# A last addition over 128 half images in 14 chunks, and a process product that alternates between the halves of its output

## The reference

```
h = tok(x)                                   # 64 x 196 x 256
h = h + attn(layernorm(h))
acts = gelu(layernorm(h) @ input_patterns.T).mean(tokens)        # 64 x 2048
input_repr = keep the 256 largest of acts, zero elsewhere
process = gelu(input_repr @ process_input_weights.T)             # 64 x 1024
top 128 of process, softmax -> mix process_values -> 64 x 128
out_acts = gelu(mixed @ output_input_weights.T)                  # 64 x 2048, keep the 256 largest
out = kept out_acts @ output_patterns                            # 64 x 256, one vector per image
h = h + out, the same vector for all 196 tokens of an image
```

## Time and profile before

| what | us |
|---|---|
| median of 3 runs (1791.88 to 1796.01) | 1794.66 |
| profiled execution, its own time | 1792.7 |
| its span, first to last instruction | 1790.7 |
| process product, on the chain | 26.75, from 1583.08 |
| first addition begins | 1739.09 |
| first store is issued | 1741.47 |
| end of the span | 1790.7 |

### The profile page before, as it was taken

One profiled execution on the slowest core, in us unless ns is written; L12 is line 12 of the kernel. 1 busy time (PEld: TensorE's weight loads), 2 busy tenths in 40 slices (PEclk: granted clock), 3 DMA queues, 4 the chain that ended last, 5 costly groups with the idle time before them and its releaser, 6 DMA issues. The chain is left out here.

```text
span 1790.7 us, 32340 instructions
## 1 busy us (share of the span) xinstructions
PE 1523.7 (85%) x10035; PEld 1461.8 (82%) x10035; DVE 1026.3 (57%) x2479; ACT 879.0 (49%) x3121; POOL 107.8 (6%) x240
## 2 busy tenths in 40 slices
PE   1479999999999999999999999999999996572133
PEld 1369999999999999999999999999999996431122
DVE  2365555555555555555555555555555443736776
ACT  1235555555555555555555555555555545511320
POOL 0010000000000000000000000000000000000000
PEclk8699999999999999999999999999999998585567
DMA  5211111111111111111111111111100002485008
GB/s 99 82 54 43 41 39 36 36 36 37 37 37 37 37 37 37 37 36 36 36 36 36 36 36 36 36 37 37 37 24 9 10 13 77 142 203 142 0 22 266
DMA packets 80357, 94.19 MB, mean 53 GB/s; under 512 B 12977, under 2 KB 78513, under 8 KB 79281
## 3 DMA queue, kind: packets, MB, share of 16 engines
q1 hardware_dynamic: 79744, 93.40, 18.8%
q10 hardware_dynamic: 576, 0.35, 0.2%
HBM read 68.01 MB, written 25.69 MB: 52 GB/s over the span
## 5 line engine op out<-in xcount | busy, mean ns | idle before, releaser
L641 ACT ACTIVATE ffn<-ffn 128x196 f32<-128x196 f32 x1024 | 332.7, 325 | 254.4 <-PE ffn L557 253.9
L557 PE MATMUL ffn<-x_t_hi,pat_w_hi 128*128 128x392 f32 x1024 | 362.0, 353 | 1.7 <-DVE x_t_lo L765 1.7
L557 PE MATMUL ffn<-x_t_lo,pat_w_hi 128*128 128x392 f32 x1024 | 350.1, 342 | 0.0
L557 PE MATMUL ffn<-x_t_hi,pat_w_lo 128*128 128x392 f32 x1024 | 348.7, 340 | 0.0
L490 PE MATMUL gen<-qkvu_w_hi,h_t_hi 128*98 128x256 f32 x768 | 216.2, 282 | 5.4 <-ACT q_t L599 5.1
L490 PE MATMUL gen<-qkvu_w_hi,h_t_lo 128*98 128x256 f32 x768 | 216.2, 282 | 0.0
L490 PE MATMUL gen<-qkvu_w_lo,h_t_hi 128*98 128x256 f32 x768 | 215.7, 281 | 0.0
L641 ACT ACTIVATION_READ_ACCUMULATOR ffn<-ffn 128x1 f32 x1024 | 196.2, 192 | 0.0
L557 PEld LDWEIGHTS ffn<-x_t_hi,pat_w_hi 128*128 128x128 f32 x1024 | 192.7, 188 | 2.0 <-DVE x_t_lo L765 2.0
L557 PEld LDWEIGHTS ffn<-x_t_lo,pat_w_hi 128*128 128x128 f32 x1024 | 193.1, 189 | 0.0
L557 PEld LDWEIGHTS ffn<-x_t_hi,pat_w_lo 128*128 128x128 f32 x1024 | 192.8, 188 | 0.0
(11 more groups left out here) (192 smaller groups left out, 2753.4 us busy)
## 6 DMA issues: line engine op xcount, KB each, us to landing
raw<-in_x_dram SPq DMA_DIRECT2D x768, 49.0 KB
h_dram<-h SPq DMA_DIRECT2D x128, 98.0 KB
process_nat<-ocess_input_weights_dram SPq DMA_DIRECT2D x8, 1024.0 KB, 4.8
process_t<-h_dram SPq DMA_DIRECT2D x4, 1568.0 KB
out_dram<-process_t SPq DMA_DIRECT2D x8, 784.0 KB
h_early<-h_dram SPq DMA_DIRECT2D x3, 1568.0 KB
out_dram<-h_early SPq DMA_DIRECT2D x6, 784.0 KB
pat_nat<-_ffn_input_patterns_dram SPq DMA_DIRECT2D x1, 2048.0 KB, 8.3
```

Source lines behind the costliest of these rows:

```text
L557: last = pe.matmul(fb[f % FFN_BANKS][:, 0:T2], a[:, d, f * P:(f + 1) * P], b[:, d, :], start=n == 0, stop=n == 3 * s.halves - 1)
L641: last = act.activation(cols, cols, ACT.Gelu, accum_out=gelu_sum[:, par, at:at + 1])
```

## The change

- The tokens of the last addition are laid out over 128 partitions. Partition p holds one half image, 98 tokens that lie side by side in DRAM. The work is cut into 14 chunks of 7 tokens, so a chunk is 128 partitions x 1792 numbers, and each partition's 7168 bytes are one run on both sides of the transfer.
- The homes hold 4, 2 and 8 chunks, in the same three buffers and behind the same waits.
- PE spreads the routed vectors once: `both_halves` is now 128 columns, each image twice, and two matmuls (high and low part) put every half image's vector on its partition in bank `rp0`. DVE reads it from that bank for all 14 chunks.
- SP loads a chunk per DMA and stores a chunk per DMA, 14 of each (before 8 and 16).
- The process product does both halves of a tile before it goes to the next tile.

```diff
-        EARLY = 3 * GROUP
-        h2_early = sb("h2_early", [s.tile, EARLY, 2 * D])
-        homes = [h2_early[:], process_nat[0:s.tile].rearrange("p a b -> p (a b)").rearrange("p (n d) -> p n d", d=2 * D),
-                 process_t[0:s.tile].rearrange("p a b -> p (a b)").rearrange("p (n d) -> p n d", d=2 * D)]
+        TOKENS = s.tokens // 2
+        CHUNK = 7
+        CHUNKS = TOKENS // CHUNK
+        EARLY = 4
+        h2_early = sb("h2_early", [P, EARLY, CHUNK * D])
+        in_nat = process_nat[:].rearrange("p a b -> p (a b)")[:, 0:2 * CHUNK * D]
+        in_turned = process_t[:].rearrange("p a b -> p (a b)")[:, 0:(CHUNKS - EARLY - 2) * CHUNK * D]
+        homes = [h2_early[:], in_nat.rearrange("p (n y) -> p n y", n=2),
+                 in_turned.rearrange("p (n y) -> p n y", n=CHUNKS - EARLY - 2)]
...
-        both_halves = sb("both_halves", [P, B], F32R)
+        both_halves = sb("both_halves", [P, B, 2], F32R)
...
-            for first in range(0, B, GROUP):
-                n, at = h2_home(first)
+            def rows(dram, g):
+                return dram.rearrange("(p t) d -> p (t d)", t=TOKENS)[:, g * CHUNK * D:(g + 1) * CHUNK * D]
+
+            for g in range(CHUNKS):
+                n, at = h2_home(g)
...
-                sp.dma_start(tiles(homes[n][:, at:at + GROUP], GROUP), rows(h2_dram, first, GROUP)).then_inc(h2_in[n], 16)
-            STORE = 4
-            for first in range(0, B, STORE):
-                n, at = h2_home(first)
-                sp.wait_ge(added, (first + STORE) // 2)
-                sp.dma_start(rows(out, first, STORE), tiles(homes[n][:, at:at + STORE], STORE)).then_inc(
-                    out_stored[first // STORE % 4], 16)
+                sp.dma_start(homes[n][:, at], rows(h2_dram, g)).then_inc(h2_in[n], 16)
+            for g in range(CHUNKS):
+                n, at = h2_home(g)
+                sp.wait_ge(added, g + 1)
+                sp.dma_start(rows(out, g), homes[n][:, at]).then_inc(out_stored[g % 4], 16)
...
-                    last = pe.matmul(out, chosen_t[:, at * P + u * B:at * P + (u + 1) * B], weights(t),
-                                     start=n == 0, stop=n == tiles - 1)
+                    for v, out in enumerate(outs):
+                        last = pe.matmul(out, chosen_t[:, at * P + u * B:at * P + (u + 1) * B], weights(t, v),
+                                         start=n == 0, stop=n == tiles - 1)
...
-            for u in range(2):
-                last = chosen_product(prod[0][half_rows(u), :], IN_T,
-                                      lambda t: process_t[:, t, u * NARROW:(u + 1) * NARROW], 0 if u == 0 else None)
-            last.then_inc(product, 1)
+            chosen_product([prod[0][half_rows(v), :] for v in range(2)], IN_T,
+                           lambda t, v: process_t[:, t, v * NARROW:(v + 1) * NARROW], 0).then_inc(product, 1)
...
-            for f in range(B // 2):
-                if f >= 4:
-                    pe.wait_ge(added, f - 3)
-                for g in range(2 * f, 2 * f + 2):
-                    one = both_halves[:, g:g + 1].to_broadcast([P, s.tile])
-                    for n, part in enumerate(routed):
-                        last = pe.matmul(prod[f % 4][0:s.tile, g % 2 * D:(g % 2 + 1) * D], one, part[:],
-                                         start=n == 0, stop=n == 1)
-                last.then_inc(spread, 1)
+            for n, part in enumerate(routed):
+                last = pe.matmul(prod[0][:, 0:D], both_halves[:].rearrange("p b u -> p (b u)"), part[:],
+                                 start=n == 0, stop=n == 1)
+            last.then_inc(spread, 1)
...
-            for f in range(B // 2):
-                n, at = h2_home(2 * f)
-                if at == 0:
-                    dve.wait_ge(h2_in[n], 16 * (homes[n].shape[1] // GROUP))
-                tiles = homes[n][:, at:at + 2].rearrange("t g (u d) -> t g u d", u=2)
-                dve.wait_ge(spread, f + 1)
-                vectors = prod[f % 4][0:s.tile, :].rearrange("t (g d) -> t g d", g=2)
-                dve.tensor_tensor(tiles, tiles, vectors.unsqueeze(2).to_broadcast([s.tile, 2, 2, D]),
+            dve.wait_ge(spread, 1)
+            for g in range(CHUNKS):
+                n, at = h2_home(g)
+                dve.wait_ge(h2_in[n], 16 * homes[n].shape[1])
+                dve.tensor_tensor(by_token(homes[n][:, at]), by_token(homes[n][:, at]), to_all(prod[0][:, 0:D]),
                                   ALU.add).then_inc(added, 1)
```

More of the change, by code:

```diff
@@ L858, in route @@
         STAGE = 2 * ROUNDS
-        GROUP = 8
         process_nat = sb("process_nat", [P, 2, s.n_in])
@@ L880, in route @@
         reached_too = sb("reached_too", [P, HALF], BF16)
-        EARLY = 3 * GROUP
         UNROLL = 4
-        h2_early = sb("h2_early", [s.tile, EARLY, 2 * D])
-        homes = [h2_early[:], process_nat[0:s.tile].rearrange("p a b -> p (a b)").rearrange("p (n d) -> p n d", d=2 * D),
-                 process_t[0:s.tile].rearrange("p a b -> p (a b)").rearrange("p (n d) -> p n d", d=2 * D)]
-        assert sum(home.shape[1] for home in homes) == B
+        TOKENS = s.tokens // 2
[7 more added lines that the diff above has]
+                 in_turned.rearrange("p (n y) -> p n y", n=CHUNKS - EARLY - 2)]
+        assert CHUNK * CHUNKS == TOKENS and sum(home.shape[1] for home in homes) == CHUNKS
         def h2_home(g):
@@ L943, in half_rows, with by_token, to_all @@
             return slice(n * B, (n + 1) * B)
+        def by_token(ap):
+            return ap.rearrange("p (t d) -> p t d", d=D)
+        def to_all(ap):
+            return ap.unsqueeze(1).to_broadcast([P, CHUNK, D])
         block = ctx.enter_context(nc.Block())
@@ L972, in _ @@
                     sp.wait_ge(product, 1)
-                sp.dma_start(tiles(homes[n][:, at:at + GROUP], GROUP), rows(h2_dram, first, GROUP)).then_inc(h2_in[n], 16)
-            STORE = 4
-            for first in range(0, B, STORE):
-                n, at = h2_home(first)
-                sp.wait_ge(added, (first + STORE) // 2)
-                sp.dma_start(rows(out, first, STORE), tiles(homes[n][:, at:at + STORE], STORE)).then_inc(
-                    out_stored[first // STORE % 4], 16)
+                sp.dma_start(homes[n][:, at], rows(h2_dram, g)).then_inc(h2_in[n], 16)
[3 more added lines that the diff above has]
+                sp.dma_start(rows(out, g), homes[n][:, at]).then_inc(out_stored[g % 4], 16)
             for n in range(4):
-                sp.wait_ge(out_stored[n], 16 * (B // STORE // 4))
+                sp.wait_ge(out_stored[n], 16 * len(range(n, CHUNKS, 4)))
         @block.gpsimd
@@ L1036, in turn_chosen, with chosen_product @@
                     last.then_inc(chosen_turned, 1)
-            def chosen_product(out, tiles, weights, done):
+            def chosen_product(outs, tiles, weights, done):
                 half = tiles // 2
@@ L1043, in chosen_product @@
                     u, at = divmod(t, half)
-                    if done is not None and n % 8 == 0:
+                    if n % 8 == 0:
                         pe.wait_ge(chosen_kept, done + n // 8 + 1)
-                    last = pe.matmul(out, chosen_t[:, at * P + u * B:at * P + (u + 1) * B], weights(t),
-                                     start=n == 0, stop=n == tiles - 1)
+                    for v, out in enumerate(outs):
+                        last = pe.matmul(out, chosen_t[:, at * P + u * B:at * P + (u + 1) * B], weights(t, v),
+                                         start=n == 0, stop=n == tiles - 1)
                 return last
@@ L1078, in _ @@
             pe.wait_ge(copied, fills + out_fills)
-            chosen_product(prod[2][0:B, 0:s.d_pv + 1], PROC_T, lambda t: values[:, t, :], 2).then_inc(product, 1)
+            chosen_product([prod[2][0:B, 0:s.d_pv + 1]], PROC_T, lambda t, v: values[:, t, :], 2).then_inc(product, 1)
             pe.wait_ge(result, 2)
@@ L1140, in _ @@
             act.wait_ge(masks_made, 6)
-            act.activation(both_halves[:], same_image[:, 0:B], ACT.Copy)
+            act.activation(both_halves[:], same_image[:, 0:B].unsqueeze(2).to_broadcast([P, B, 2]), ACT.Copy)
             for n in range(STAGE):
```

## The result

The changed kernel takes 1768.01 us, against 1794.01 before on the same chip: a ratio of 0.9847 (95% interval 0.9823 to 0.987), 26 us faster. (One execution of it took 2637 us with PE at a mean clock of 0.55; the ratio leaves it out, and the median hardly feels it.) The forecast was 1766 and faster, with a range of 1762 to 1775. The profiled execution took 1768.29 us, its span 1766.6.

A forecast was written before the change was run, and what follows sets the result against it. It took the process product on the chain of waits and the stream of stores at the tail as the bounds. Terms of -11.8, -0.2, -0.4 and -16.2 us sum to -28.6, giving 1766 us, range 1762 to 1775.

The forecast's parts named there:

- What bounds the kernel: In the route, the process product sits alone on the chain of waits; the tail is bound by the stores.
- Step 1: Process product: alternating halves pair two instructions per step, 33 steps, 26.75 to 15.0 us, a term of -11.8 us.
- the seam rows: Profile rows between the product's two passes, showing extra weight loads per 0.43 us step; they would allow 32 steps, 14.6 us.
- Steps 2 and 3: Spread of vectors, 128 matmuls to 2, -0.2 us; additions 1.93 us each, first store waiting for one, -0.4 us.
- not the bound: Claim that DVE's additions, delivering 475 GB/s, outpace anything the transfers did in the trace.
- Step 4: Stream of stores at the tail: 410 GB/s instead of 279, 47.5 to 31.3 us, a term of -16.2 us.
- The rival of a lower ceiling for writes near 361: Stores limited to 361 GB/s: stream 35.6 us, 4.3 us more, 1770 us; chance 0.17.
- The rival that only partitions count: Stores at 279 to 325 GB/s, stream 46 to 39.5 us, 1774 to 1781 us; chance 0.10.
- The slower rival: Scattered writes at 98 KB pitch fall to 193 GB/s, stream 66.6 us, 1801 us in all; chance 0.03.
- The sum: All terms together -28.6 us: span 1790.7 to 1762.1, profiled execution 1764.1, median 1766 us.
- the third case: In the list of chances, stores at 279 to 325 GB/s, 1774 to 1781 us; chance 0.10.
- the second: In the list of chances, the write ceiling near 361 GB/s, 1770 us; chance 0.17.

The follow-up runs named there:

- tail alone: The changed kernel with the process product in two passes again, lower half then upper: median 1778.03 us, ratio 0.9903 to the kernel before.
- short first store: The changed kernel with chunk 0 added and stored in two pieces, 2 and 5 tokens: median 1763.39 us, ratio 0.9829 to the kernel before.
- product alone: The kernel before with only the process product alternating between halves: median 1783.63 us, ratio 0.9938 to the kernel before.
- 112 partitions: The changed kernel with tokens on 112 partitions, 16 chunks of 7 tokens, runs of 7 KB: median 1769.48 us, ratio 0.986 to the kernel before.
- PE busy ahead of product: The changed kernel with five extra matmuls into a free bank before the process product: median 1761.94 us, ratio 0.9819 to the kernel before.
- few columns: The short first store kernel, with every addition after the first piece covering one token only: median 1763.94 us, ratio 0.9826 to the kernel before.

## Why the prediction was right

**What bounds the kernel** held: between the kernel with the tail alone and the changed kernel the product differs by 11.05 us and the other two pieces by 0.3 or less, so the product's time comes off the end one for one, and the end is the stream of stores.

**Step 1** had -11.8, measured -11.05 in the profile, and -10.9 to -12.1 over all runs with paired halves and no extra matmuls. The pairing was right. Two things inside it were off and partly cancelled. There are 32 steps and not 33 (13.9 us at the upper level is 32 x 0.43 and the drain), as the seam rows had allowed; by the prediction's own terms that is 14.7 us and not the 14.6 it gives. And the steps at the lower level are 2 to 4.5, not always 2: the changed kernel's profile had some 4, which is (15.70 - 13.9) / 0.43. When the level rises differs from one execution to the next.

**Steps 2 and 3** had -0.2 and -0.4. From the product's end to the first addition it is 0.6 less, of which 0.2 are the two matmuls and 0.26 the output product's clock; the first store comes 0.33 earlier. The additions follow each other at 1.93 us, as worked out. (The 1.13 us that this starts from is right, but comes from the starts in the earlier trace rows, 12.4 us for 11 steps; 10 in 11.10 would be 1.11.) That they are "not the bound" holds for the stream as a whole, but not for its start, as the short first store showed.

**Step 4** had a rate of 410 and -16.2; measured 416 and -16.5. The row of 8 KB loads was the right neighbour: stores ran at nearly the rate of those loads (422). The rival of a lower ceiling for writes near 361 falls with the 416. The Trainium skill ("DMA: Bandwidth & Descriptors", Bandwidth) gives some 358 GB/s as the limit of the memory for one core; here one core alone stored at 416, so that limit did not bind. The rival that only partitions count is refuted by 349 against 416. Why 98 partitions are slow the prediction did not say beyond the 14 engines, and it stays open in part. The slower rival, a fall to 193 GB/s at a pitch of 98 KB, did not appear at all; in the changed kernel even the loads of h2 from the same places ran at 412 to 434 GB/s (1606 to 1620 us).

**The sum.** -11.05 - 0.6 - 0.33 - 16.5 = -28.5 for the route, forecast -28.6. That sum came out so close partly by luck, since the smaller misses cancel: +0.75 in step 1, -0.4 in step 2, +0.07 in step 3, -0.3 in step 4. The 4.4 us that the profile gives back lie before the route, whose first transposes start at 1506.78 instead of 1502.41. The prediction has no term for that; three runs of the changed kernel lie between 1763.45 and 1768.29, and a median 2 us above the forecast is within this scatter. (In the chances, it is the upper end of the third case and not of the second that lies outside 1762 to 1775.) PE's clock as the tower starts, before and after:

```profile
50.00:100.00 50.00, 24.00 (x129) 22.54 (x130) 21.49 (x43) 15.17 (x31) 2.54 (x6) 0.74 0.27 80
100.00:150.00 50.00, 41.95 (x301) 40.52 (x300) 30.41 (x73) 22.69 (x59) 3.28 (x7) 0.97 0.19 55
```

```profile
50.00:100.00 50.00, 23.65 (x119) 22.53 (x120) 21.75 (x43) 14.87 (x29) 2.54 (x6) 0.67 0.27 79
100.00:150.00 50.00, 42.10 (x271) 40.68 (x271) 28.68 (x69) 19.86 (x48) 3.28 (x7) 0.84 0.18 51
```

The clock was 0.84 instead of 0.97 there, and fewer matmuls got done. The tower's end can be read from the first transposes of the route. In the eleven profiles they start at 1501.9 to 1502.8 in five (before, product alone, tail alone, 112 partitions, PE busy ahead of product), with 0.74 or 0.75 in the first window and 0.90 to 0.97 in the second. They start at 1503.5 to 1505.5 in four with 0.67 and 0.93 to 0.96, at 1503.6 in the run with few columns with 0.74 and 0.95, and at 1506.8 in the changed kernel with 0.67 and 0.84. Taken over both windows, the clock is the lower the later the tower ends, in ten of the eleven; only the run with few columns is out of order. That the clock is the whole of the 4.4 us is not shown, and what makes it differ between executions stays open.

## What to carry to other kernels

A transfer between DRAM and SBUF is worth laying out over all 128 partitions with runs of several KB: here the partitions alone took 10.5 us off a stream of 47.5, the run length alone 3.4, and both 16.5, so the second pays most once the first is done. It is not enough that the partitions divide evenly over the transfer engines: 112 partitions kept all engines busy and were still 7.6 us slower than 128. Two float32 products of 64 columns cost about the time of one if they are issued in turn for the two halves of PSUM (13.9 to 15.9 us instead of 26.75), and a seam in an existing trace can show that before it is tried. When one stream follows another at nearly its own rate, starting it earlier gains little until the feeder is faster too (0.2 us with the additions whole, some 1.2 with few columns).

## What was not expected of the hardware

- A few useless matmuls in an idle gap of PE made the work behind it cheaper: 13.9 to 14.0 us for the product against 14.7 to 15.9 in all other runs with paired halves.
- The tower, the same in all kernels here, ended up to 5 us apart from one execution to the next, mostly along with PE's clock between 50 and 150 us. That is more than the smallest effects looked for here, so those were read from pieces of the chain, not from medians.
